# Two-phase attention and expert kernel: the P V result kept as channels by tokens, its softmax sums inverted by way of DMA

## What is computed

```
# first block, for each of 4 batches, 16 heads of 32 channels
xn = rms_norm(x, g_norm) * (1 + scale) + shift
q, k, v = split(xn @ W_qkv);  q, k = rms_norm(q, g_q), rms_norm(k, g_k)
o = softmax(q k^T * d**-0.5) @ v            # per head
x1 = o + o @ W_out
# second block: latent attention with rotary parts, causal
o = softmax(causal(q k^T * d**-0.5)) @ v     # per head
h = x1 + o @ o_w, then rms norm, a shared expert and 2 of 7 routed experts, added
```

## Time and profile before

| | us |
|---|---|
| median of 3 runs | 1297.6 |
| lowest and highest | 1291.22, 1298.75 |
| span of the profiled execution | 1289.1 |
| TensorE busy in it | 1169.7 |
| VectorE, ScalarE, GpSimd busy | 744.4, 572.3, 290.7 |

### The profile page before, as it was taken

One profiled execution on the slowest core, in us unless ns is written; L12 is line 12 of the kernel. 1 busy time (PEld: TensorE's weight loads), 2 busy tenths in 40 slices (PEclk: granted clock), 3 DMA queues, 4 the chain that ended last, 5 costly groups with the idle time before them and its releaser, 6 DMA issues.

```text
span 1289.1 us, 18670 instructions
## 1 busy us (share of the span) xinstructions
PE 1169.7 (91%) x6059; PEld 825.7 (64%) x6059; DVE 744.4 (58%) x1807; ACT 572.3 (44%) x1248; POOL 290.7 (23%) x244
## 2 busy tenths in 40 slices
PE   5979999999999889999999989989999999999970
PEld 5745555665566446557767757766657888888850
DVE  6565675477545856666565575566364774444433
ACT  3324464345443555455465454455264753222210
POOL 1313122100210031001011200200124464555530
PEclk9979999999999999999999999999899999999995
DMA  7064243125311732352284264265357744555559
GB/s 255 33 180 131 65 136 112 50 86 184 99 50 58 225 107 57 99 189 88 88 259 149 86 234 122 84 201 176 86 186 232 262 152 105 109 108 113 115 134 331
DMA packets 88127, 178.42 MB, mean 138 GB/s; under 512 B 12609, under 2 KB 23265, under 8 KB 86497
## 3 DMA queue, kind: packets, MB, share of 16 engines
q1 hardware_dynamic: 79216, 156.90, 37.4%
q0 software_dynamic: 8512, 19.93, 8.2%
q10 hardware_dynamic: 304, 0.40, 0.2%
HBM read 110.86 MB, written 65.27 MB: 137 GB/s over the span
## 4 chain that ended last, share of the span: by engine, by line
PE 77%; DVE 8%; DMA 5%; ACT 4%; issue 3%; SPq 1%; POOL 0%; DVEq 0%; ACTq 0%; POOLq 0%
PE psum L862 14%; PE psum L681 9%; PE psum L682 8%; PE psum L683 8%; PE psum L846 6%; PE psum L825 6%; PE psum L690 4%; PE psum L940 4%; PE psum L942 4%; PE psum L941 4%; PE psum L967 2%; PE psum L969 2%; PE psum L968 2%; PE psum L909 2%; PE psum L772 2%
## 5 line engine op out<-in xcount | busy, mean ns | idle before, releaser
L1174 ACT ACTIVATE probs<-psum 128x512 f32<-128x512 f32 (+3 forms) x512 | 257.3, 517 | 231.5 <-PE psum L849 120.6
L825 PE MATMUL psum<-stack 96*128 96x512 f32 (+3 forms) x512 | 210.2, 416 | 8.6 <-DMA stack<-split_s 4.0
L1583 DVE TENSOR_REDUCE nmax<-psum 128x1 f32<-128x512 f32 x256 | 170.5, 684 | 77.0 <-PE psum L825 73.2
L846 PE MATMUL psum<-stack 97*128 97x512 f32 (+3 forms) x512 | 197.3, 386 | 16.8 <-ACT probs L1174 15.4
L862 PE MATMUL psum<-probs,vals 128*33 128x512 f32 (+3 forms) x1024 | 209.4, 531 | 0.0
L1586 DVE CUSTOM_DVE_ANT_0 psum<-psum,causal 128x128 f32<-128x128 f32 (+3 forms) x256 | 123.0, 501 | 21.0 <-PE psum L825 19.4
L825 PEld LDWEIGHTS psum<-stack 96*128 96x128 f32 x512 | 100.0, 196 | 46.3 <-issue 23.7
L846 PEld LDWEIGHTS psum<-stack 97*128 97x128 f32 x512 | 99.0, 193 | 40.0 <-ACT probs L1174 25.8
L862 PEld LDWEIGHTS psum<-probs,vals 128*33 128x33 f32 x1024 | 49.8, 112 | 99.6 <-issue 65.5
L681 PE MATMUL psum<-w_hi,xh 128*128 128x512 f32 (+1 forms) x256 | 95.4, 373 | 4.2 <-DVEq L1449 2.5
L682 PE MATMUL psum<-w_hi,xl 128*128 128x512 f32 (+1 forms) x256 | 93.6, 366 | 0.0
(11 more groups left out here) (238 smaller groups left out, 2338.0 us busy)
## 6 DMA issues: line engine op xcount, KB each, us to landing
stack<-split_s SPq DMA_DIRECT2D x378, 128.0 KB, 3.0
split_s<-split SPq DMA_DIRECT2D x64, 512.0 KB, 3.0
xt<-in_x_dram SPq DMA_DIRECT2D x4, 1024.0 KB, 5.2
x_s<-yt SPq DMA_DIRECT2D x4, 1024.0 KB, 5.0
xt<-x_s SPq DMA_DIRECT2D x4, 1024.0 KB, 4.8
yt<-in_x_dram SPq DMA_DIRECT2D x4, 1024.0 KB, 5.6
res<-x_s SPq DMA_DIRECT2D x4, 1024.0 KB, 8.2
acc_s<-yt SPq DMA_DIRECT2D x4, 1024.0 KB, 6.0
```

The costliest lines, as they stand in the source:

```text
L825: sq.filled(nc.tensor.matmul(psum[:, sq.bank(M), 0:n], st[:, 0, t * P:(t + 1) * P], st[:, 1, 0:n], start=True, stop=True), M)
L846: last = nc.tensor.matmul(psum[:, bank, lo:S], st[:, 1, t * P:(t + 1) * P], st[:, 0, lo:S], start=True, stop=not masked)
L1174: sk.cleared(nc.scalar.activation(probs[:, M % NX, lo:S], psum[:, sk.bank(M), lo:S], ACT.Exp, scale=SCALE), M)
L1583: sq.cleared(V.tensor_reduce(out, psum[:, sq.bank(M), :], AX.X, ALU.max, negate=True), M)
```

## The change

The result of P V is no longer turned. Pairs are regrouped: in a group of four heads, pair 0 has heads 0 and 2, pair 1 heads 1 and 3 (`head_of`, `slot_of`), so that after the copy their rows can be put together as the 128 channels of a group in their own order. For each chunk c (two pairs, 128 channels):

- `pair_out` copies an even pair to `raw` (still named `o_chunk` in the trace), an odd one to `ev` (`o_pair`).
- `take_sums` on SP: two small transfers per pair spread each head's row of 512 sums over 32 partitions of 16 (`rden`, now named `prob_sums`, 128x16), and two more per odd pair move its heads' rows into `raw`.
- `inverse`: VectorE inverts the 128x16. `store_inverse` writes it to DRAM (`inverse_s`); `load_inverse` waits for that to land and reads each head's row back over 32 partitions, four loads (`inverse_sums`).
- `divide`: VectorE multiplies `raw` by it. `o_split`: ScalarE copies `o_hi`, GpSimd subtracts for `o_lo`.

In steps of a batch, with p the odd pair: sums at 8p+11, inverse at 8p+14, its store at 8p+15, its loads at 8p+17, divide at 8p+20, split at 8p+21 (for chunk 0 at 8p+31). The last two pairs of the last batch keep the way before (`by_turns`). 31 chunks and 62 pairs are changed. The buffer `oc` is single and lies where `inv` does.

```diff
+def by_turns(k, p):
+    return k == NB - 1 and p >= NPR - 2
...
+    for b in (i, k):
+        past = STEPS_H * (k - b)
+        for p in range(NPR if b >= 0 else 0):
+            if not by_turns(b, p):
+                keys = [(11, ("sums", b, p))]
+                if p % 2:
+                    c = p // 2
+                    keys += [(14, ("inverse", b, c)), (15, ("inverse_out", b, c)), (17, ("inverse_in", b, c)),
+                             (20, ("divide", b, c)), (21 if c else 31, ("o_split", b, c))]
...
-        put((5,), [("back", i, NPR - 1)])
-        put((8,), [("turn_o", i, NC - 1)])
...
-    put(range(13, 64, STEPS_P), each("back", k, NPR - 1))
-    put((38, 46, 57), each("turn_o", k, NC - 1))
+    if k == NB - 1:
+        put((61,), [("back", k, NPR - 2)])
...
+def head_of(p, side):
+    return p // 2 * HPG + p % 2 + 2 * side
...
+            def take_sums(k, p):
+                n = NPR * k + p
+                o.wait_read(sp, n)
+                src = ev if p % 2 else raw[:, p // 2 % 2, :]
+                for side in range(2):
+                    row = HALF * side + DH
+                    to = HALF * (p % 2) + DH * side
+                    sp.dma_start(rden[to:to + DH, :], src[row:row + 1, :]).then_inc(sums_ld[p % 2], 16)
+                if p % 2:
+                    sp.wait_ge(sums_ld[0], 32 * (n // 2 + 1))
+                    for side in range(2):
+                        to = HALF * side + DH
+                        sp.dma_start(raw[to:to + DH, p // 2 % 2, :],
+                                     ev[HALF * side:HALF * side + DH, :]).then_inc(heads_mv, 16)
+            def store_inverse(k, c):
+                sp.wait_ge(inv_ok, NC * k + c + 1)
+                sp.dma_start(inv_s.rearrange("o a (d n) -> (o a d) n", d=DH), rden[:, :]).then_inc(inv_st, 16)
+            def load_inverse(k, c):
+                sp.wait_ge(inv_st, 16 * (NC * k + c + 1))
+                if NC * k + c:
+                    sp.wait_ge(o_div, NC * k + c)
+                for n in range(HPG):
+                    sp.dma_start(inv[DH * n:DH * n + DH, :],
+                                 inv_s[n % 2, n // 2:n // 2 + 1, :].broadcast_to([DH, S])).then_inc(inv_ld, 16)
...
                     if t == 0:
-                        for c in (NC - 2, NC - 1):
-                            ring.wait_read(pe, ("turn_o", j, c))
+                        pe.wait_ge(o_lo, sum(b <= j for b, c in DIVIDED))
+                        if j == LAST:
+                            ring.wait_read(pe, ("turn_o", j, NC - 1))
...
             def pair_out(p):
                 act.wait_ge(pv_mm, STEPS_P * (p + 1))
-                if p >= 2:
-                    ring.wait_full(act, ("back", *divmod(p - 2, NPR)))
-                o.cleared(copy(ev[0:OW, p % 2, :], psum[0:OW, o.bank(p), :]), p)
+                if p % 2:
+                    act.wait_ge(sums_ld[1], 32 * (p // 2))
+                    act.wait_ge(heads_mv, 32 * (p // 2))
+                    to = ev
+                else:
+                    if p >= 4:
+                        act.wait_ge(o_lo, p // 2 - 1)
+                    to = raw[:, p // 2 % 2, :]
+                o.cleared(copy(to[0:OW, :], psum[0:OW, o.bank(p), :]), p)
...
+                elif kind == "inverse":
+                    c, = at_
+                    for n in range(2):
+                        dve.wait_ge(sums_ld[n], 32 * (NC * j + c + 1))
+                    V.reciprocal(rden[:, :], rden[:, :]).then_inc(inv_ok, 1)
+                elif kind == "divide":
+                    c, = at_
+                    dve.wait_ge(heads_mv, 32 * (NC * j + c + 1))
+                    dve.wait_ge(inv_ld, 64 * (NC * j + c + 1))
+                    V.tensor_tensor(raw[:, c % 2, :], raw[:, c % 2, :], inv[:, :], ALU.mult).then_inc(o_div, 1)
```

More of the change, by code:

```diff
@@ L150, in head_step, with slot_of @@
     p, n = divmod(m, STEPS_P)
-    return k, 2 * p + n % 2, n // 2
+    return k, p, n % 2, n // 2
+def head_of(p, side):
+    return p // 2 * HPG + p % 2 + 2 * side
+def slot_of(p, side):
+    return p % 4 * 2 + side
 def max_turn(M):
@@ L188 @@
 HI_NO = numbered(lambda x: x[0] in ("kv_d", "q_d", "turn_o", "x2") or x[0] in ("x", "turn") and x not in VALUE_NO)
+DIVIDED = [(k, c) for k in range(NB) for c in range(NC) if not by_turns(k, 2 * c)]
 NV = len(VALUE_NO)
@@ L284, in build @@
         rsh = small("rsh", [P, 2, NT * 2 * H])
-        nmax, rden = small("nmax", [P, 2, 2 * NT]), small("rden", [P, 2, NT, 2])
+        nmax, rden = small("nmax", [P, 2, 2 * NT]), small("prob_sums", [P, HPG * NT])
         rwh, rwl = small("rwh", [P, NC, NE], F32R), small("rwl", [P, NC, NE], F32R)
@@ L330, in build @@
         oh, ol = rest("o_hi", [P, NC, S], F32R), rest("o_lo", [P, NC, S], F32R)
-        oc = rest("o_chunk", [P, 2, NT, P])
-        ev = rest("o_pair", [P, 2, S])
+        raw, inv = rest("o_chunk", [P, 2, S]), rest("inverse_sums", [P, S])
+        oc = at("o_by_tokens", rest.where - 4 * S, [P, NT, P])
+        ev = rest("o_pair", [P, S])
         mrow = rest("max_rows", [P, P], F32R)
@@ L400, in build @@
         pv_mm = sem("pv_products")
+        sums_ld, heads_mv = [sem(f"prob_sums_loaded{i}") for i in range(2)], sem("odd_pair_moved")
+        inv_ok, inv_st, inv_ld = sem("sums_inverted"), sem("inverse_sums_stored"), sem("inverse_sums_loaded")
+        o_div, o_hi, o_lo = sem("o_divided"), sem("o_hi_ready"), sem("o_lo_ready")
         y1_st = sem("x1_stored")
@@ L485, in load_pair @@
                 src = split_s[q // 2].rearrange("(h p) c t -> p c h t", p=DH)
-                heads, at_ = slice(q % 2 * 2, q % 2 * 2 + 2), p % 4 * 2
+                heads, at_ = slice(q % 2, HPG, 2), p % 4 * 2
                 for n, (stored, parts) in enumerate(((k_st, (2, 2, 3)), (q_st, (0, 1, 0)))):
@@ L573, in _ @@
                         place_rows(max_turn(k * STEPS_H + m))
+                    for key in BESIDE[k].get(m, ()):
+                        if key[0] == "sums":
+                            take_sums(*key[1:])
+                        elif key[0] == "inverse_out":
+                            store_inverse(*key[1:])
+                        elif key[0] == "inverse_in":
+                            load_inverse(*key[1:])
                     for key in BESIDE[k].get(m - 2, ()):
@@ L778, in beside @@
                         ring.wait_read(pe, ("back", j, p))
-                    turn(key, lambda t: oc[:, c % 2, t, :])
+                    turn(key, lambda t: oc[:, t, :])
                 elif kind == "out":
@@ L818, in scores @@
             def scores(M):
-                k, h, t = head_step(M)
+                k, q, side, t = head_step(M)
                 if M % STEPS_P == 0:
@@ L823, in scores @@
                 n = (t + 1) * P if phase(k) == 2 else S
-                st = stack[0:XSTACK, :, h % NSTK]
+                st = stack[0:XSTACK, :, slot_of(q, side)]
                 sq.filled(nc.tensor.matmul(psum[:, sq.bank(M), 0:n], st[:, 0, t * P:(t + 1) * P], st[:, 1, 0:n],
@@ L844, in scores_t @@
                 bank = sk.bank(M)
-                st = stack[0:XSTACK + 1, :, h % NSTK]
+                st = stack[0:XSTACK + 1, :, slot_of(q, side)]
                 last = nc.tensor.matmul(psum[:, bank, lo:S], st[:, 1, t * P:(t + 1) * P], st[:, 0, lo:S],
@@ L852, in pv @@
             def pv(M):
-                k, h, t = head_step(M)
-                p, side = M // STEPS_P, h % 2 * HALF
+                k, q, side, t = head_step(M)
+                p, at_ = M // STEPS_P, side * HALF
                 if M % STEPS_P == 0:
@@ L861, in pv @@
                 lo = t * P if phase(k) == 2 else 0
-                nc.tensor.matmul(psum[side:side + VW, o.bank(p), lo:S], vals[k % 2][:, t, h, :], probs[:, M % NX, lo:S],
+                nc.tensor.matmul(psum[at_:at_ + VW, o.bank(p), lo:S], vals[k % 2][:, t, head_of(q, side), :], probs[:, M % NX, lo:S],
                                  start=(t == 0), stop=(t == NT - 1)).then_inc(pv_mm, 1)
@@ L1101, in beside @@
                         hi_of(key, split[:, {"q": 0, "k": 2}[c], :])
-                elif kind == "turn_o":
+                elif kind == "o_split":
                     c, = at_
@@ L1107, in beside @@
                         ring.wait_full(act, ("out", j - 1, NT - 1))
+                    act.wait_ge(o_div, NC * j + c + 1)
+                    copy(oh[:, c, :], raw[:, c % 2, :]).then_inc(o_hi, 1)
+                elif kind == "turn_o":
+                    c, = at_
                     hi_of(key, oh[:, c, :])
@@ L1172, in _ @@
                     act.wait_ge(pv_mm, M - NX + 1)
-                lo = head_step(M)[2] * P if phase(k) == 2 else 0
+                lo = head_step(M)[3] * P if phase(k) == 2 else 0
                 sk.cleared(nc.scalar.activation(probs[:, M % NX, lo:S], psum[:, sk.bank(M), lo:S], ACT.Exp, scale=SCALE), M)
@@ L1577, in maximum @@
             def maximum(M):
-                k, h, t = head_step(M)
+                k, q, side, t = head_step(M)
                 sq.wait_full(dve, M)
```

(2 more changed lines are left out.)

19 lines of the change are left out of this document (15 added, 4 removed).

## The result

| | kernel before | changed kernel |
|---|---|---|
| median, first measurement | 1296.06 us | 1281.01 us (1280.03 to 1282.27) |
| ratio, first measurement | | 0.9903 (0.9874 to 0.9931) |
| ratio, second measurement, nine runs | | 0.9931 (0.9904 to 0.9958) |
| span of the profiled execution | 1289.1 us | 1278.3 us |

The change makes the kernel faster by 0.7 to 1.0%, 9 to 15 us. The forecast was 21.4 us, to 1276, so the sign and the range held, and the gain is 0.4 to 0.7 of what was forecast; between the two profiled executions it is 10.8 us of span, half of it. The profiled execution took 1280.03 us, 1.7 more than its span.

A forecast was written before the change was run, and what follows sets the result against it. TensorE was taken to bound the attention stretch. Terms: -36.4 for turns gone, +5 staying as waiting, +5 at batch 4, +5 at other places, -21.4 us, taking the median from 1297.6 to 1276; range 1256 to 1295.

The forecast's parts named there:

- turns gone: TensorE's queue: 62 back turns 20.3 us, 31 turn_o turns 13.3, waits for VectorE's remainder 2.8; gross 36.4 us saved.
- what of it stays as waiting: TensorE's existing waits for ScalarE's exponentials and split grow as work before them goes: 5 us lost, bounds 0 and 12.
- batch 4, step 54: Inverses' store queues behind wo_raw and ln_row on SP, delaying loads, divide and split: 5 us added, bounds 0 and 9.
- other places of the trip: Loads of x at step 6 (batches 4, 5), stores of x2 at step 54 (batches 5 to 7): 1 us each, 5 together.
- TensorE sets the pace: Attention stretch, 98 to 968 us: TensorE busy 817.1 of 870 us, so instructions off its queue count by their chain place.
- The steady state at nothing: Ordinary chunks: the round trip takes 13.2 us and nine masked steps 15 us, so it just fits; no cost counted.
- The rule of the Trainium skill: Divide and GpSimd subtraction exclude each other: 31 x 0.02 us by the rows; port rival at most 20 us, 1287, chance 0.03.
- the full gain: Rival: stalls behind big transfers already hidden, nothing turns to waiting; -36.4 us, time 1261, chance 0.23.
- The freed time: Rival: ring banks and hand-overs through ScalarE and VectorE set the step, TensorE idles more; -6 us, time 1291, chance 0.13.
- The late trip in every chunk: Rival: load_inverse holds SP and the divide holds VectorE in every chunk; +16 us, time 1314, chance 0.09.
- the bound of 1%: Whole kernel: measurement tells about 1%, 13 us, from no change; faster means below 1284.6, chance 0.72; within 1%, 0.19; slower, 0.09.

The follow-up runs named there:

- without the trip: Changed kernel without sums out, moved rows, reciprocal, store and loads; divide multiplies by 1, so output is not normalized and lacks odd pairs' heads: 1264.54 us, 0.9794.
- GpSimd's queue: Changed kernel with all eleven DMAs of the round trip issued by GpSimd in the same steps, not by SP: 1329.56 us, 1.0296.
- the run in which VectorE does not wait: Changed kernel with all DMAs kept, no reciprocal, SP waiting for the sums and storing them as they are, divide multiplying by 1: 1272.06 us, 0.9851.

## Why the prediction was right in sign and range, and too large in size

The forecast's sum can be set beside the profiled executions (the other execution of the changed kernel ended 6.9 us later, so each line holds to a few us):

| term | forecast | in the traces |
|---|---|---|
| turns gone | -36.4 | not seen apart |
| what of it stays as waiting | 5 | 13, if the line above is right |
| both together | -31.4 | -23.4 (without the trip) |
| batch 4, step 54 | 5 | 5 to 6 |
| other places of the trip | 5 | 7 |
| sum | -21.4 | -10.8 |

- *TensorE sets the pace, and what is taken from its chain is gained*: right. Without the trip the kernel is 26 us faster in the medians, and up to the last pair of the heads 29, 0.47 us a pair as against 31.4 / 62 = 0.51.
- *"What of it stays as waiting", 5 us*: this is the term that was most mis-sized. It is 10 us in the medians (36.4 less 26) and 13 in the traces. The prediction put it near the lower end of its bounds, 0 and 12, because TensorE's idle share was small. But 5.7 us are given back behind the last pair of the heads, and 3 at the weights of the second block in batch 2; the kernel without the trip shows both.
- *The steady state at nothing*: not contradicted. After 31 pairs the kernel without the trip is ahead by 12.0 us and the changed one by 11.2 and 7.0. The landings were shorter than the row taken for them (5.9 against 9 us), and the moved rows' issue longer (0.59 against 0.43), which changes nothing.
- *Batch 4, step 54, 5 us*: the place and the mechanism were right to the instruction, and the size too. Issue at 647.4, landing 8.3 us later, loads until 657.4, divide at 659.2. Against the kernel without the trip the changed one falls back by 8.6 us at that row-maxima issue, and has 3.4 of them back one pair later.
- *The other places, 1 us each, 5 in all*: too small, some 7 us in the traces, and more in the medians, where the whole trip costs 14 to 18 us and not 10. Most of it falls at one stall in the last batch, behind the shared expert's weights (917.4), which was not on the list: the kernel without the trip gains 3.2 us on the changed one at the row-maxima issue behind it and 1.9 at the next. The stall behind the last store of x2 was on the list. The one behind the weights of the second block, in batch 2, was not (the sums land 6.9 us late at 431.9), but as the kernel without the trip stalls there too, it is hardly a cost of the trip. The one early in batch 7 has no big transfer in front at all.
- *The clock*: no term at all. It is not a cost beside those in the table but a part of them. The granted clock over the span fell from 0.970 to 0.955:

```profile
core 0: 1289.1 us, clock 0.970
...
core 0: 1278.3 us, clock 0.955
```

  With two levels, 2.4 and 1.2 GHz, a mean of 0.970 over 1289 us is 77 us at the lower one, and 0.955 over 1278 us is 115. Some 36 to 38 us of each lie at the very end, where TensorE has no more work and they cost nothing. Cut into windows of 10 us, the heads (100 to 960 us) have 24 us at the lower level before, 65 in the changed kernel (72 in its other execution) and 44 without the trip. The same stretch in one piece, before and without the trip:

```profile
98.00:953.00 855.00, 803.13 (x4273) 529.89 (x4273) 520.09 (x1375) 421.60 (x959) 119.20 (x112) 0.99 0.40 125
...
98.00:953.00 855.00, 798.00 (x4035) 519.48 (x4035) 505.31 (x1266) 433.06 (x985) 168.00 (x148) 0.97 0.42 130
```

  In the changed kernel's chain a block of eight L930 products takes 1.84 us at a granted clock of 1.00, and 3.56 at 0.50, right after the stall at 431.9:

```profile
333.63 1.84 PE psum L930 x8
...
441.66 3.56 PE psum L930 x8
```

  A microsecond at the lower level thus costs up to half of it where TensorE is the bound: up to 20 us in the changed kernel's heads, and up to 10 of them are there without any trip. The clock fell in or right behind stalls: in windows of 1 us it goes to 0.5 from 435 (TensorE all but idle from 433.4 to 437), from 657 (busy 0.5 of 5 us from 655) and from 879 (idle from 877.4), and stays there 7 to 10 us, while TensorE is busy again for most of them. So such a stall costs more than its length. Not every fall stands behind a window that is half idle: the one at 880 follows one that is busy 7.16 of 10 us.
- *The rule of the Trainium skill* ("SBUF — State Buffer", "SBUF: two separate sides": a VectorE instruction with two SBUF inputs and a GpSimd instruction that reads SBUF exclude each other): the trace agrees. The divide has 692 ns median, 1449 at most, and a mean of 835:

```profile
L1610 DVE TENSOR_TENSOR o_chunk<-o_chunk,inverse_sums 128x512 f32<-128x512 f32 x31 | 25.9, 835 | 26.5 <-DMA inverse_sums<-inverse_s 26.5
L1387 POOL TENSOR_TENSOR o_lo<-o_chunk,o_hi 128x512 fp32r<-128x512 f32 x31 | 41.3, 1332 | 199.5 <-ACT o_hi L1094 199.5
```

  That is 31 x (0.835 - 0.692) = 4.4 us of VectorE, not 0.6, and still not 20. Set beside GpSimd's timeline, the seven divides of 1.16 us and more all overlap a GpSimd instruction that was under way when they started, and six of them end 0.55 us after it; the other 24, of 0.67 to 0.69 us, overlap none. The partners are not the subtraction behind the divide, which the prediction had in mind, but other work of the unmasked batches, such as:

```profile
145.43 1.04 POOL L1374 TENSOR_TENSOR vs<-qk 128x512 f32<-128x512 f32 x1 [2.66 <-ACT qk L1094]
...
145.60 1.42 DVE L1610 TENSOR_TENSOR o_chunk<-o_chunk,inverse_sums 128x512 f32<-128x512 f32 x1
```

  All seven lie in the first half of the heads, where no cost of the trip is seen.
- *The rivals*: the full gain (1261) would have been the kernel without the trip (1264.5). The freed time did not turn to waits for ScalarE in general: the 26 us are there. The late trip in every chunk is what GpSimd's queue gives. By the bound of 1%, the change lies at its edge or within: 0.97% in the first measurement and 0.69% in the second, where the prediction gave 0.72 to more than 1%.

What stays open: how the 14 to 18 us of the trip divide between VectorE's waiting, SP's hold and the extra traffic; what the later split is worth without GpSimd's divide; and what share the clock, `res` and the tile rows have in the 4 to 6 us given back behind the last pair.

## What to carry to other kernels

When compute work is replaced by a chain of small DMAs, the median landing prices the easy chunks and says little of the rest. List every transfer above half a megabyte on the same queue, and every long run of issues, and put each of the small ones' waits beside it; most of the stalls stand right behind them, and moving a big transfer helps only if it does not land ahead of another small one. Let the engine that waits for a landing be one whose queue nobody needs: the divide on an idle engine, with a later split, gave 8 us with no change in any DMA. Look at the granted clock before you explain a few us. And follow a gain to the end of the program: part of it can be lost where the next stage's loads begin.

## What the runs showed of the hardware

- Small transfers land faster than the 128 KB ones: 1.7 us for 32 pieces of 64 bytes within SBUF, 1.8 for 8 KB to DRAM, 2.4 for one row read over 32 partitions. Behind 1.25 MB on the queue the same 8 KB took 8.3.
- The same small DMAs issued by GpSimd cost it some 170 us more of busy time in the stretch (333 against 164 us, for 341 DMAs, 0.5 us each), and the store landed in 3.2 us.
- A VectorE multiplication with both inputs in SBUF that starts while a GpSimd instruction runs ends 0.55 us after it, and takes 1.16 to 1.45 us in place of 0.69. With one SBUF input, in the run in which VectorE does not wait, most such cases end 0.28 us after it, and take up to 1.16 in place of 0.42.
- After the three stalls of TensorE looked at closely (at 433, 655 and 877 us of the changed kernel) the granted clock was 0.50 for 7 to 10 us, and a block of eight products took 3.56 us in place of 1.84.
- Two executions of one program differed by 6.9 us of span (1278.3 and 1285.2) with clocks of 0.955 and 0.950. In the heads they had 65 and 72 us at the lower level; half of the difference is some 4 us. For this kernel, a good part of the spread between runs can be the clock's.
